# Ternary feed-forward weights as float32r operands in the last layer, with x and the gelu results split in two halves

## The reference

```
def _ternary(w):
    scale = jnp.maximum(jnp.mean(jnp.abs(w)), 1e-08)
    w_t = jnp.clip(jnp.round(w / scale), -1.0, 1.0)
    return w + jax.lax.stop_gradient(w_t - w)
h = jnp.einsum('bsd,fd->bsf', x, _ternary(W1)) + b1
h = jax.nn.gelu(h, approximate=False)
out = jnp.einsum('bsf,df->bsd', h, _ternary(W2)) + b2
```

## Time and profile before

| what | us |
|---|---|
| median of 3 runs | 1797.4 |
| lowest and highest | 1796.44, 1804.03 |
| the profiled execution, its own time | 1797.52 |
| its span, first to last instruction | 1795.7 |
| layer 3, first GpSimd operation to last add | 1491.36 to 1788.79 |

### The profile page before, as it was taken

The page is one execution under the profiler, slowest core; times in us unless marked ns, Lnnn a source line. Parts: engine busy times, 40 slices in busy tenths (PEclk is TensorE's granted clock), DMA queues, the critical chain, the costliest instruction groups (busy, mean ns, idle before and its releaser), DMA issues. The chain is left out here.

```text
span 1795.7 us, 22762 instructions
## 1 busy us (share of the span) xinstructions
PE 1704.2 (95%) x8614; PEld 1001.2 (56%) x8614; DVE 1005.5 (56%) x1660; ACT 830.0 (46%) x1022; POOL 385.5 (21%) x306
## 2 busy tenths in 40 slices
PE   7899999997989989999999999999999997999996
PEld 4232222223544437777878787877878773444443
DVE  4555555544774435455545445455554447888885
ACT  4667777775443324333434333333434334445442
POOL 1000000000690003021121203020111204655552
PEclk8799999998889989999999999999999998999998
DMA  2222222223007620000000000000000010000001
GB/s 77 51 48 48 48 48 48 48 48 123 1 4 180 145 50 1 1 1 2 1 1 1 1 1 1 1 1 1 1 1 2 1 58 0 1 0 1 1 0 47
DMA packets 19128, 49.15 MB, mean 27 GB/s; under 512 B 784, under 2 KB 1680, under 8 KB 18128
## 3 DMA queue, kind: packets, MB, share of 16 engines
q1 hardware_dynamic: 19024, 47.73, 11.4%
HBM read 45.23 MB, written 2.36 MB: 27 GB/s over the span
## 5 line engine op out<-in xcount | busy, mean ns | idle before, releaser
L498 ACT ACTIVATE probs<-ps_ring 128x1024 f32<-128x1024 f32 x256 | 245.9, 1024 | 88.6 <-PE ps_ring L735 85.6
L1791 PEld LDWEIGHTS ps_o<-v,probs 128*128 128x128 f32 x2048 | 235.3, 192 | 31.0 <-issue 24.9
L1791 PE MATMUL ps_o<-v,probs 128*128 128x129 f32 x2048 | 248.1, 278 | 1.8 <-ACT probs L1516 1.2
L1516 ACT ACTIVATE probs<-ps_ring 128x1024 f32<-128x1024 f32 x128 | 126.8, 1023 | 212.1 <-PE ps_ring L1772 212.0
L1597 DVE TENSOR_REDUCE negmax<-ps_o 128x2 f32<-128x1024 f32 x64 | 78.5, 1226 | 137.0 <-PE ps_o L1747 137.0
L749 PE MATMUL ps_o<-probs,v 128*32 128x512 f32 x1024 | 138.3, 614 | 0.9 <-DVE o_sb L559 0.9
L1509 ACT ACTIVATE xn<-ps_ring,pack 128x512 f32<-128x512 f32 x64 | 40.5, 684 | 162.6 <-PE ps_ring L1356 162.6
L1971 POOL TENSOR_TENSOR rs<-r,state 128x512 f32<-128x512 f32 x64 | 86.0, 1346 | 115.1 <-DVE state L2118 114.8
L1610 DVE RECIPROCAL rden<-ps_o 128x2 f32<-128x2 f32 x128 | 21.5, 168 | 143.2 <-PE ps_o L1791 143.2
L735 PEld LDWEIGHTS ps_ring<-q_stack,k_stack 32*128 32x128 f32 x512 | 31.8, 185 | 123.4 <-issue 98.4
L2118 DVE TENSOR_TENSOR_SCAN state<-decay,state,kv 128x511 f32<-128x511 f32 x64 | 91.7, 1434 | 6.5 <-issue 1.1
(11 more groups left out here) (378 smaller groups left out, 3413.3 us busy)
## 6 DMA issues: line engine op xcount, KB each, us to landing
cwb<-combine_by_expert SPq DMA_DIRECT2D x8, 2048.0 KB
score<-score_by_expert SPq DMA_DIRECT2D x7, 2048.0 KB, 14.0
pack<-pack_dram SPq DMA_DIRECT2D x1, 3840.0 KB, 15.2
pack<-pack_dram SPq DMA_DIRECT2D x1, 2507.0 KB, 8.8
x<-x_in SPq DMA_DIRECT2D x2, 1024.0 KB, 6.4
out<-x SPq DMA_DIRECT2D x1, 2048.0 KB, 6.3
score<-score_by_expert SPq DMA_DIRECT2D x1, 1536.0 KB, 13.5
pack<-pack_dram SPq DMA_DIRECT2D x1, 1479.0 KB, 6.4
```

The costliest lines, as they stand in the source:

```text
L498: nc.scalar.activation(probs[n % 3][:, 2 * half:2 * half + 2, :], ps, ACT.Exp, scale=float(HD0) ** -0.5).then_inc(read, 1)
L1516: nc.scalar.activation(probs[:, n % 2, m, :, :], ps, ACT.Exp).then_inc(read, 1)
L1791: last = nc.tensor.matmul(ps_o[:, i, k * (D + 1):(k + 1) * (D + 1)], probs[:, (b * PAIRS + p) % 2, m, j, queries], v[:, m, h, :], start=(m ...
```

## The change

- The ternary form of W1 and W2 is written as float32r into the tiles `tern[0]` and `tern[1]`, as the difference of two comparisons; the two operations that formed `w + (w_t - w)` go. The parts of `hid` serve as scratch.
- x of a sequence (`xn`) is split: ScalarE copies it to `xn_high` (float32r) between `take_y` and `take_v`; GpSimd subtracts to get `xn_low` (`low_x`) at the end of its turn, behind `step_back`. Each `up` is two float32r matmuls (low, then high) instead of one whole product.
- Each gelu is done twice from the same PSUM slot: once to `hid` in float32, once to `hid_high` in float32r. GpSimd subtracts to get `hid_low` (`low_h`), four times per turn: two behind times_r 4, one ahead of times_r 6, one behind it. Each `down` is two float32r matmuls (high, then low).
- The counts of `rk_ready` (3 per sequence instead of 2) and `mixed_ready` (5 instead of 4) follow. `up` of a sequence waits for `low_x`, each second half of `down` for its `low_h`, and each gelu for the `low_h` of the sequence before on the same part.

```diff
--- before.py
+++ after.py
@@ -1893,7 +1893,8 @@
         vw = w.tensor[:, first_v:first_v + (1 + HD3) * P]
         vw_high, vw_low = sb("vw_high3", [P, (1 + HD3) * P]), sb("vw_low3", [P, (1 + HD3) * P])
         yc, sq, rstd, o = (sb(f"{n}3", [P, T]) for n in ("yc", "sq", "rstd", "o"))
-        hid = sb("hid3", [P, FT, T])
+        hid, hid_high, hid_low = (sb(f"{n}3", [P, FT, T]) for n in ("hid", "hid_high", "hid_low"))
+        xn_high, xn_low = sb("xn_high3", [P, 2, T]), sb("xn_low3", [P, 2, T])
         mag, tern = ([sb(f"{name}3_{n}", [P, FF]) for n in range(2)] for name in ("mag", "tern"))
         row_sum = sb("row_sum3", [P, 2])
         bound = sb("bound3", [P, 6])
@@ -1914,7 +1915,7 @@
         ruk_ready, vu_ready = sem("ruk_ready"), sem("vu_ready3")
         scanned, rs_ready, picked = sem("scanned3"), sem("rs_ready"), sem("picked3")
         squared, rstd_ready, o_ready = sem("squared3"), sem("rstd_ready3"), sem("o_ready3")
-        up_done, gelued = sem("up_done3"), sem("gelued3")
+        up_done, gelued, hid_low_ready = sem("up_done3"), sem("gelued3"), sem("hid_low_ready3")
         out_done, x_added = sem("out_done3"), sem("x_added3")
         block = ctx.enter_context(nc.Block())
 
@@ -1939,14 +1940,10 @@
         def ternary_weight(nc_engine, eng, n, done):
 
             m = w[FF_WEIGHTS[n]]
-            nc_engine.tensor_scalar(mag[n][:, :], m, bound[:, 4 + n:5 + n], None, ALU.is_lt)
-            nc_engine.tensor_scalar(tern[n][:, :], m, bound[:, 2 + n:3 + n], None, ALU.is_gt)
+            nc_engine.tensor_scalar(hid[:, 2 * n, :], m, bound[:, 4 + n:5 + n], None, ALU.is_lt)
+            nc_engine.tensor_scalar(hid[:, 2 * n + 1, :], m, bound[:, 2 + n:3 + n], None, ALU.is_gt)
             eng.drain()
-            nc_engine.tensor_tensor(tern[n][:, :], tern[n][:, :], mag[n][:, :], ALU.subtract)
-            eng.drain()
-            nc_engine.tensor_tensor(tern[n][:, :], tern[n][:, :], m, ALU.subtract)
-            eng.drain()
-            nc_engine.tensor_tensor(m, m, tern[n][:, :], ALU.add).then_inc(done, 1)
+            nc_engine.tensor_tensor(single(tern[n][:, :]), hid[:, 2 * n + 1, :], hid[:, 2 * n, :], ALU.subtract).then_inc(done, 1)
 
         @block.gpsimd
         def _(pool):
@@ -1965,10 +1962,20 @@
                 n = b * HD3 + j
                 pool.wait_ge(scanned, n + 1)
                 if j == 0:
-                    pool.wait_ge(rk_ready, 2 * b + 1)
+                    pool.wait_ge(rk_ready, 3 * b + 1)
                 if n >= 4:
                     pool.wait_ge(picked, n - 3)
                 nc.gpsimd.tensor_tensor(rs[:, j % 4, :], r[:, b % 2, :], st[:, j, :], ALU.mult).then_inc(rs_ready, 1)
+
+            def low_x(a):
+                pool.wait_ge(rk_ready, 3 * a + 3)
+                nc.gpsimd.tensor_tensor(single(xn_low[:, a % 2, :]), xn[:, at(a)], xn_high[:, a % 2, :], ALU.subtract
+                                        ).then_inc(mixed_ready, 1)
+
+            def low_h(b, t):
+                pool.wait_ge(gelued, b * FT + t + 1)
+                nc.gpsimd.tensor_tensor(single(hid_low[:, t, :]), hid[:, t, :], hid_high[:, t, :], ALU.subtract
+                                        ).then_inc(hid_low_ready, 1)
 
             nc.gpsimd.memset(zero[:, :], 0.0)
             pool.drain()
@@ -1988,11 +1995,15 @@
                     add_x(a, 2, "k")
                 if b is not None:
                     times_r(b, 4)
+                    low_h(b, 0)
+                    low_h(b, 1)
                     times_r(b, 5)
                 if a is not None:
                     add_x(a, 4, "g")
                 if b is not None:
+                    low_h(b, 2)
                     times_r(b, 6)
+                    low_h(b, 3)
                     times_r(b, 7)
                 if a is not None and a + 1 < B:
                     step_back(a + 1)
@@ -2001,6 +2012,8 @@
                     pool.wait_ge(scale_step, BOUND)
                     ternary_weight(nc.gpsimd, pool, 1, down_ternary)
                     pool.drain()
+                if a is not None:
+                    low_x(a)
 
         @block.scalar
         def _(act):
@@ -2020,7 +2033,12 @@
             def gelu(b, t):
                 n = b * FT + t
                 act.wait_ge(up_done, n + 1)
-                nc.scalar.activation(hid[:, t, :], ps_f[:, t % 2, :], ACT.Gelu, bias=w["b1_3"][:, t:t + 1]).then_inc(gelued, 1)
+                if b:
+                    act.wait_ge(hid_low_ready, (b - 1) * FT + t + 1)
+                else:
+                    act.wait_ge(down_ternary, 1)
+                nc.scalar.activation(hid[:, t, :], ps_f[:, t % 2, :], ACT.Gelu, bias=w["b1_3"][:, t:t + 1])
+                nc.scalar.activation(single(hid_high[:, t, :]), ps_f[:, t % 2, :], ACT.Gelu, bias=w["b1_3"][:, t:t + 1]).then_inc(gelued, 1)
 
             def decays(a):
                 ps, read = filled(act, ("lb_dd", a))
@@ -2078,6 +2096,7 @@
                 if b is not None:
                     take_y(b)
                 if a is not None:
+                    nc.scalar.activation(single(xn_high[:, a % 2, :]), xn[:, at(a)], ACT.Copy).then_inc(rk_ready, 1)
                     take_v(a)
 
         @block.vector
@@ -2103,7 +2122,7 @@
                                         ).then_inc(xv_ready, 1)
 
             def weigh_rk(b):
-                dve.wait_ge(rk_ready, 2 * b + 2)
+                dve.wait_ge(rk_ready, 3 * b + 2)
                 nc.vector.scalar_tensor_tensor(ruk[:, :], r[:, b % 2, :], w["u"], k[:, b % 2, :], ALU.mult, ALU.mult).then_inc(ruk_ready, 1)
 
             def scan(b, j):
@@ -2240,7 +2259,11 @@
                 n = b * FT + t
                 if n >= 2:
                     pe.wait_ge(gelued, n - 1)
-                nc.tensor.matmul(ps_f[:, t % 2, :], w["W1_3"][:, t * P:(t + 1) * P], xn[:, at(b)], start=True, stop=True).then_inc(up_done, 1)
+                if t == 0:
+                    pe.wait_ge(mixed_ready, 5 * b + 5)
+                up_weight = single(tern[0][:, t * P:(t + 1) * P])
+                nc.tensor.matmul(ps_f[:, t % 2, :], up_weight, single(xn_low[:, b % 2, :]), start=True, stop=False)
+                nc.tensor.matmul(ps_f[:, t % 2, :], up_weight, single(xn_high[:, b % 2, :]), start=False, stop=True).then_inc(up_done, 1)
 
             def down(b, t):
                 if t == 0 and b:
@@ -2248,7 +2271,10 @@
                 if t == 0 and b == 0:
                     pe.wait_ge(down_ternary, 1)
                 pe.wait_ge(gelued, b * FT + t + 1)
-                nc.tensor.matmul(ps_x[:, :], w["W2_3"][:, t * P:(t + 1) * P], hid[:, t, :], start=(t == 0), stop=False)
+                down_weight = single(tern[1][:, t * P:(t + 1) * P])
+                nc.tensor.matmul(ps_x[:, :], down_weight, single(hid_high[:, t, :]), start=(t == 0), stop=False)
+                pe.wait_ge(hid_low_ready, b * FT + t + 1)
+                nc.tensor.matmul(ps_x[:, :], down_weight, single(hid_low[:, t, :]), start=False, stop=False)
 
             def project_out(c):
                 pe.wait_ge(o_ready, c + 1)
@@ -2293,7 +2319,7 @@
                     pick(b, 1)
                     up(b, 3)
                 if a is not None:
-                    pe.wait_ge(mixed_ready, 4 * a + 1)
+                    pe.wait_ge(mixed_ready, 5 * a + 1)
                     multiply(("la_dd", a), (w["la_d"], mixed["d"][:, :]))
                 if b is not None:
                     scan_input(b, 5)
@@ -2313,14 +2339,14 @@
                     pick(b, 4)
                 if a is not None:
                     for n, name in enumerate("rk"):
-                        pe.wait_ge(mixed_ready, 4 * a + 2 + n)
+                        pe.wait_ge(mixed_ready, 5 * a + 2 + n)
                         multiply((name, a), (w[f"{name}W"], mixed[name][:, :]))
                 if b is not None:
                     down(b, 0)
                     pick(b, 5)
                     down(b, 1)
                 if a is not None:
-                    pe.wait_ge(mixed_ready, 4 * a + 4)
+                    pe.wait_ge(mixed_ready, 5 * a + 4)
                     multiply(("g", a), (w["gW"], mixed["g"][:, :]))
                 if b is not None:
                     pick(b, 6)
```

## The result

| kernel | median us | lowest to highest | runs |
|---|---|---|---|
| before, beside these runs | 1800.26 | 1796.44 to 1804.03 | 4 |
| with the change | 1824.28 | 1823.32 to 1829.35 | 4 |

The change makes the kernel slower, by 24 us or 1.4%: the ratio is 1.0144 (95% interval 1.0117 to 1.017). The forecast was 1823.6 us.

A forecast was written before the change was run, and what follows sets the result against it. TensorE was taken as the bound, with the VectorE-GpSimd loop close behind. On 1797.5 us, 0.7 + 6 x 2.9 + 2.0 + 6 x 1.0 = +26.1 gave 1823.6 us; own range 1804 to 1838, with rival 3 1794 to 1838.

The forecast's parts named there:

- first turns: First turn of the last layer: VectorE 1.5 us earlier, but alternation with GpSimd costs over 2 later; sum +0.7 us.
- five full turns: Last layer's equal-length middle turns, six in the forecast: each +2.9 us from blocking and +1.0 from TensorE's clock.
- the last full turn, the last turn and the tail: End of the last layer: full turn +2.9 and +1.0 us, last turn +2.0, tail unchanged.
- The walk: Full turn followed in queue order, VectorE and GpSimd blocking each other: last scan 2.9 us later, turn 36.8, not 33.9.
- the wait before add_out: VectorE's 0.90 us wait in a full turn goes; the sixth scan then waits for rs(4) and ends 0.15 later.
- Rival 2: Full turns: new GpSimd operations block nobody, the scan loop gains only the 0.90 us wait; 9 less, 1788.5 us; chance 0.08.
- The clock: TensorE's clock falls to 1.2 GHz around its waits for rs(6) and rs(7): +1.0 us per full turn, bounds 0 and 2.8.

The follow-up runs named there:

- keep_busy: Changed kernel plus ten unread single products per turn on TensorE, in its waits for GpSimd's rs: 1821.04 us, ratio 1.0118 to the kernel before.
- fill_for_low_h: Changed kernel with each low_h replaced by two GpSimd constant fills that read nothing, second down product taking hid_high: 1803.84 us, ratio 1.0014 to the kernel before.
- low_h_twice: Changed kernel with each low_h subtraction done twice, the first into an unused tile: 1865.95 us, ratio 1.0368 to the kernel before.
- up_only: Changed kernel with only the up half of the change: down products whole as before, one gelu, no low_h: 1797.65 us, ratio 0.999 to the kernel before.
- no_low_h: Changed kernel without the four low_h subtractions per turn, second down product taking hid_high again: 1799.06 us, ratio 0.9987 to the kernel before.
- high_only: Changed kernel without both low halves: one float32r product for each two, one gelu, no low_x or low_h: 1797.61 us, ratio 0.999 to the kernel before.

## Why the prediction was right

The forecast was 26.1 us for the layer; it was 24.1. Step by step, measured in the layer alone:

| step of the sum | forecast | measured |
|---|---|---|
| up to the third interpolation (first turns) | +0.7 | -0.3 (56.1 against 56.3 us) |
| five full turns to the last interpolation | +19.5 | +18.4 (188.2 against 169.8) |
| the last full turn, the last turn and the tail | +5.9 | +6.0 (77.2 against 71.3) |

**The walk.** It gave 36.8 us for a turn without clock loss; keep_busy has 36.79 to 36.81 in five turns, and the change itself 36.78 in the turn shown. The last scan was to end 34.1 us behind the turn's interpolation (1683.9 less 1649.8): it ends at 1698.18, 34.1 behind 1664.11. The single delays are there too: low_x on the first scan, rs(4) on the sixth, rs(5) on the seventh, then mixed_v, xv_low and the last scan, each within 0.1 us of the walk. That this blocking, and not the number of operations, is the cause is shown by fill_for_low_h: with GpSimd's queue about as full, but of operations that read nothing, xv_low takes 0.69 us, not 1.59, and the turn is 2.1 us shorter. low_h_twice shows it only in part, since its turns end on GpSimd's queue. The prices are near those of the walk but not the same: -2.8 us for four operations taken away (-3.4 expected), +4.7 for four added (+4.3 expected).

**What TensorE's saving is worth.** The walk took the wait before add_out as the only thing that a faster TensorE could give, and nearly all of it as lost on rs(4). up_only and no_low_h (34.0 us a turn) show both. Rival 2's sum, with 0.9 us a turn to gain, was built on the same wait without that second step, and would have been wrong even without the four low_h: even high_only, with 5 us less on TensorE and no low_x, gains 0.25.

**The clock.** Forecast +1.0 a turn; three of the five measured turns are 1.2 to 1.5 us over 36.8 and two are at 0 and 0.1, in the mean 0.84. That the clock is the cause is settled by keep_busy. The path was right in part. The clock fell in every full turn, and not only in 4 of 6, as the expectation for keep_busy has it; it costs time only where it is still at half when the next turn's value products run. These are the turns that start at 1587.89, 1625.87 and 1700.89, where it was at half until 1590.9, 1628.45 and 1703.55. There the first kv waits 1.1 to 1.7 us, not only the third as the prediction had it. The forecast of a mean was near, but no steady loss of 1.0 us stands behind it. The waits were of 1.9 and, in the turn shown, 1.5 us, not of 2.1 each. The second is the shorter for products at half clock ahead of it; where the clock held between the two, in the turn that starts at 1550.98, it is 1.93.

**The kernel before** was taken to have turns of 33.9 us throughout; the first of the five has 34.44, 0.6 more. That is half of the 1.1 us by which the five turns came out below the forecast; the rest is mostly the clock.

**Too high** by a little, 1.0 us, was the term of the first turns. Their first half gained more than the 1.5 us forecast: the second interpolation comes 21.5 us after the layer's start and not 23.8, 2.3 earlier. VectorE's dropped operations bring its mixes 1.6 forward, as forecast. The other 0.7 is a wait of its gate for ScalarE (0.62 us) that is gone. The likely cause, which no run isolates, is that before, TensorE's products ahead of it ran at half clock (1509.05 to 1512.45), behind a wait of 2.08 us that the change shortens to 0.54. The second half then lost 2.1, as walked ("over 2").

In absolute terms the agreement of 0.7 us (1824.28 against 1823.6) is better than the parts, and that is luck: the kernel before stood at 1797.4 when the forecast was made and at 1800.3 beside the change, and that makes up for the 2 us too much in the sum.

## What to carry to other kernels

Where VectorE and GpSimd both work on operands in SBUF, count their time together: an operation that moves to GpSimd's idle time was free here only where VectorE did nothing with two SBUF inputs, no cast and no tensor_scalar beside it (the gate's tensor_scalar took 1.33 us beside add_x of d and 0.55 without it). Walk one steady turn in queue order with that rule before spending work on the engine that looks like the bound: here the saving on TensorE was worth next to nothing in a full turn, and three additions moved the other way, from GpSimd to TensorE, took 15 us off the layer of high_only and 16.5 off that of the changed kernel. The float32r products are what made room for them on TensorE. A short wait on an engine can be what lets another pass; taking it away may give nothing.

## What was not expected of the hardware

- The granted clock fell to half near the end of all six full turns of the change: in five of them 0.5 to 1.3 us after the end of the first wait (1.91 to 1.95 us), in one only after a second wait of 1.93 us. It came back before the next interpolation in two of them and after it in three; behind the sixth no interpolation follows. Before the change a single wait of 1.65 us (ahead of the product of ruk in the second turn) had left it at 1.00. A wait's length alone did not decide it: in high_only TensorE waits 2.4 us for rs(7) in every turn from the third interpolation on, and the clock fell at the end of two of these six waits and held through four.
- The start of the last layer moved between 1490.6 and 1499.3 us in executions whose programs are the same up to there, while in the trace of before the last four of the five full turns are within 0.02 us of one another. That is about as wide as the runs of one kernel scatter (7.6 us for before). That it is the larger part of this scatter is likely but not shown, since each kernel has one trace.
